# Two-layer attention and mixture-of-experts kernel: six shared tiles behind the routed ones, with layer 1's first normalised rows, its first products and the second batch's gather among them; low halves of layer 1's weights on POOL

## The chip, the cores and the metric

One core of one Trainium2 chip. The time is device microseconds of the whole kernel, from one launch. Engines are named as in the profile: PE (TensorE matmul), PEld (its weight loads), DVE (VectorE), ACT (ScalarE), POOL (GpSimd), SP (SyncE, which only issues DMAs here).

## What is computed

Four blocks in a row, on 8 batches of 512 tokens with 256 features:

```
x  = L0_attn(x)       # layer norm, 16-head causal attention
x  = x + L0_ffn(...)  # 8 routed experts, top 2 of a softmax router, plus one shared expert:
                      #   h = silu((x @ w1 + b1) * (x @ w3 + b3));  h @ w2 + b2   (hidden 352)
x  = L1_attn(x)       # z = sigmoid(x Wz + bz); a = 1 - z; b = z * (x Wh + bh)
                      # h_t = a_t h_(t-1) + b_t (a scan along tokens); sigmoid(h Wg + bg) * h
x  = L1_ffn(x)        # sigmoid router with groups, top 2 of 8 experts on a 128-wide latent,
                      # relu^2 experts, plus a shared relu^2 MLP of 1024
```

Products of fp32 accuracy are made from fp16 pairs: each operand is split in a high half (a rounded copy) and a low half (the rest), and three matmuls replace one: high by high, high by low, low by high.

## The kernel before, in words

Three phases, each a block of its own with one program per engine; a block ends when every engine has come to its end, and the next one starts behind that common barrier.

The first phase (L0_attn, router) runs until about 455 us. The second (`experts_phase`) handles tiles of 256 tokens. `over_experts` sets the order for all engines: 11 tiles of the shared expert (`HEAD_TILES`), then some 20 routed tiles, expert by expert, then 5 more shared tiles (`TAIL_TILES`, stages 0 to 4). A tile is the same work everywhere: PE `gate_up` (36 matmuls into banks 0 to 2, m = 0, 1, 2), ACT `bias1`, DVE `gated` (the product, which frees the bank for the next tile), ACT `hidden` (silu twice), DVE `hidden_lo`, and in the next tile's turn PE `out` of this one (18 matmuls), then DVE `total_y` and an SP store. PE's `gate_up(i, m)` waits for DVE's `gated(i-1, m)`.

Around this order lie pieces for others:
- In the head tiles DVE and POOL write one-hot matrices (`place` on DVE, L1638, eight per tile in tiles 0 to 7; `in_lane`, L1431, 64 on POOL, then two more, L1434). PE multiplies them (`table`, L1798) ahead of the last two head tiles, and the result, `tokens`, tells POOL which rows to gather for each routed tile: `fetch` (L1400 copies the tokens, L1404 gathers) and `move` (L1412, to `xg`), which PE transposes (`x_transposes`, L1730) one tile ahead, inside the last head tile for the first routed one.
- Layer 1's weights (8208 columns, `pack32`) come in 12 parts of 684 columns, loaded in the head tiles. ACT makes the high half of a part (`pack_part`, L1503), DVE the low half (L1631), in head tiles 1 to 10 and in tail stages 0 and 1.
- In the tail, POOL gathers the first batch's routed rows (L1453, eight gathers) once the last routed tile is stored. DVE adds them to the rows in `front.x2` and takes statistics (`first_sums` in stages 2 and 3, `first_statistics` in stage 3). POOL makes the inverse deviation (L1456 to L1461), ACT normalises (`first_normalise`, L1526, in stage 4 between `bias1` and `hidden`), PE transposes (`front_transposes`, L1778, in stage 4 behind `out` of stage 3). The tails of the engines: PE `out` of stage 4; ACT `xT_hi` (L1533); DVE `xT_lo` (L1668), `total_y` of stage 4, `first_slots(1)` (L1643, L1644).

The third phase (`layer1_phase`) runs eight batches, one `step` each. A step begins on PE with the router's logits (24 narrow matmuls, into l_sc on ACT), the latent `lat` (6 wide ones), `z0` (6), then `h0`, `z1`, `h1`, eight `up` products, and so on. On POOL, step b first gathers the routed rows of batch b+1 (L2018); DVE adds them in its step b (L2168). SP starts with three small loads of biases, waits for the last stored tile and loads the rows of the next batch (L1984).

## Time and profile before

| | |
|---|---|
| time, median of 3 runs | 1202.05 us (1201.46 to 1204.6) |
| profiled execution, its time | 1203.08 us |
| its span in the trace | 1201.3 us |
| PE busy | 1115.7 us (93%) |
| DVE busy | 894.9 us (74%) |
| ACT busy | 676.0 us (56%) |
| POOL busy | 531.2 us (44%) |
| mean granted clock of TensorE | 0.979 of full |

The page lists busy time by engine, the span in 40 slices, the chain of work that ended last, and groups of instructions. PE is busy nearly everywhere; what remains are places where it waits, and where its granted clock is at half. The answers below are cut to such places. A row of a timeline gives start, duration, engine, line, operation, what it writes and reads, how many are merged, and in brackets how long the engine stood idle before it and who released it. Matmuls overlap: one of 256 columns is shown with 0.27 us, the next begins 0.109 us later.

### The profile page before, as it was taken

How to read it: one execution, taken by the hardware profiler on the slowest of the kernel's cores; microseconds unless marked ns; L12 is line 12 of the kernel's file. 1: busy time of each engine (PE TensorE's matmuls, PEld its weight loads, DVE VectorE, ACT ScalarE, POOL GpSimd, SP SyncE). 2: the span in 40 equal slices, each digit the busy share in tenths (PEclk: the TensorE clock that was granted, in tenths of full speed). 3: DMA queues.
4: the chain of work that ended last, by engine and by line, in shares of the span. 5: the costliest groups of instructions: out<-in, count | busy, mean ns of one | idle time of the engine just before them, and what ended most of it. 6: DMA issues, size and time to landing. Idle time of an engine off the chain costs nothing. (4 is left out here: it accounts for less than half of the span.)

```text
span 1201.3 us, 26766 instructions
## 1 busy us (share of the span) xinstructions
PE 1115.7 (93%) x8899; PEld 747.5 (62%) x8931; DVE 894.9 (74%) x2219; ACT 676.0 (56%) x1464; POOL 531.2 (44%) x743
## 2 busy tenths in 40 slices
PE   6799999999999888998999999997999999999998
PEld 3345555555555437887998888983656646546555
DVE  5878797888887847975656667674886876877876
ACT  2355565565555554665656566654654654664653
POOL 6442433434333226854444343323646546447414
PEclk9799999999999999999999999997999999999999
DMA  6448435455334405755332453452241341331211
GB/s 162 108 90 227 99 68 110 98 98 107 62 85 93 82 18 186 218 162 155 113 101 79 126 159 122 127 155 74 89 141 35 107 140 35 105 106 63 95 45 62
DMA packets 105044, 129.36 MB, mean 108 GB/s; under 512 B 14976, under 2 KB 92736, under 8 KB 103936
## 3 DMA queue, kind: packets, MB, share of 16 engines
q1 hardware_dynamic: 93712, 109.08, 34.1%
q0 software_dynamic: 6912, 18.88, 5.6%
q10 hardware_dynamic: 4336, 0.34, 0.3%
q8 instruction: 46, 0.75, 0.3%
q14 instruction: 38, 0.31, 0.1%
HBM read 84.70 MB, written 43.38 MB: 107 GB/s over the span
## 5 line engine op out<-in xcount | busy, mean ns | idle before, releaser
L544 ACT ACTIVATE p<-bank 128x384 f32<-128x384 f32 (+1 forms) x384 | 191.6, 531 | 185.2 <-PE bank L957 136.1
L769 DVE TENSOR_REDUCE neg_max<-bank 128x1 f16<-128x384 f32 (+3 forms) x352 | 219.7, 640 | 65.9 <-PE bank L945 56.5
L463 POOL TENSOR_SCALAR_AFFINE_SELECT p<-p 128x256 f32<-128x256 f32 x256 | 104.5, 412 | 233.8 <-ACT p L544 233.1
L942 PE MATMUL bank<-k_stack,q_stack 96*128 96x384 f16 (+3 forms) x512 | 133.2, 312 | 23.4 <-DVE neg_max L769 13.0
L1404 POOL DMA_INDIRECT fetched<-xn_dram,token_now x80 | 81.2, 1014 | 42.9 <-POOL token_now L1400 30.7
L2033 POOL TENSOR_TENSOR up_lo<-up_sq,up_hi 128x512 f16<-128x512 f32 x32 | 43.8, 1398 | 120.8 <-ACT up_hi L2090 120.8
L2044 POOL TENSOR_TENSOR he_lo<-he_sq,he_hi 128x512 f16<-128x512 f32 x64 | 79.9, 1270 | 36.6 <-ACT he_hi L2133 36.6
L957 PE MATMUL bank<-q_stack,k_stack 97*128 97x512 f16 (+1 forms) x256 | 91.5, 360 | 3.1 <-ACT p L544 1.5
L1488 ACT ACTIVATE a<-xbank,b 128x256 f32<-128x256 f32 (+1 forms) x126 | 58.7, 469 | 52.3 <-PE xbank L151 48.8
L1576 DVE TENSOR_TENSOR h_lo<-h,h_hi 128x256 f16<-128x256 f32 x159 | 68.0, 431 | 24.3 <-ACT h_hi L1497 23.4
L975 PE MATMUL bank<-p,v_aug 128*32 128x512 f32 (+3 forms) x1024 | 83.9, 447 | 0.8 <-DVE o_rows L749 0.8
L942 PEld LDWEIGHTS bank<-k_stack,q_stack 96*128 96x128 f16 x512 | 45.2, 99 | 61.3 <-DVE neg_max L769 40.7
L149 PE MATMUL ybank<-l_xT_hi,pack_hi 128*128 128x512 f16 x208 | 79.9, 384 | 2.6 <-DVE up_sq L2247 2.6
L150 PE MATMUL ybank<-l_xT_lo,pack_hi 128*128 128x512 f16 x208 | 79.8, 384 | 0.0
L151 PE MATMUL ybank<-l_xT_hi,pack_lo 128*128 128x512 f16 x208 | 79.8, 384 | 0.0
L1495 ACT ACTIVATE h<-prod 128x256 f32<-128x256 f32 x159 | 64.8, 408 | 24.6 <-DVE prod L1570 19.5
L1570 DVE SCALAR_TENSOR_TENSOR prod<-xbank,b,a 128x256 f32<-128x256 f32 (+1 forms) x126 | 58.5, 477 | 24.8 <-ACT a L1488 20.3
L945 PE MATMUL bank<-mask_qk,identb 128*128 128x128 bf16 (+1 forms) x321 | 76.7, 239 | 0.0
L149 PE MATMUL ybank<-pack_hi,up_hi 128*128 128x256 f16 x256 | 69.8, 273 | 0.0
L150 PE MATMUL ybank<-pack_lo,up_hi 128*128 128x256 f16 x256 | 69.8, 273 | 0.0
L151 PE MATMUL ybank<-pack_hi,up_lo 128*128 128x256 f16 x256 | 69.8, 273 | 0.0
L2018 POOL DMA_INDIRECT rows_k<-y_routed_dram,slot x56 | 56.5, 1008 | 27.7 <-issue 15.9
(344 smaller groups left out, 3379.9 us busy)
## 6 DMA issues: line engine op xcount, KB each, us to landing
w_bc<-wT_dram SPq DMA_DIRECT2D x8, 2048.0 KB, 8.3
y_routed_dram<-y SPq DMA_DIRECT2D x37, 256.0 KB
w<-in_w SPq DMA_DIRECT2D x10, 704.0 KB
pack<-in_pack SPq DMA_DIRECT2D x12, 342.0 KB, 4.4
xr<-in_x SPq DMA_DIRECT2D x8, 512.0 KB, 6.9
xn_dram<-xn SPq DMA_DIRECT2D x8, 512.0 KB, 3.0
qk_hi_dram<-qk_hi SPq DMA_DIRECT2D x16, 256.0 KB, 2.7
qk_lo_dram<-qk_lo SPq DMA_DIRECT2D x16, 256.0 KB, 2.9
```

Source lines behind the costliest of these rows:

```text
L149: pe.matmul(out, hi_a(c), hi_b(c), start=first and x == 0, stop=False)
L150: pe.matmul(out, hi_a(c), lo_b(c), start=False, stop=False)
L151: mm = pe.matmul(out, lo_a(c), hi_b(c), start=False, stop=last and x == n - 1)
L463: pool.affine_select(out=diagonal, in_=diagonal, pattern=[[0, 2], [1, P]], compare_op=ALU.is_ge, fill=0.0, base=0, channel_multiplier=-1). ...
L544: act.activation(p32[:, s // GH % 2, s % GH, cols], s_bank[n][:, 0:cols.stop - cols.start], ACT.Exp).then_inc(p_exp.sem, 1)
L769: dve.tensor_reduce(neg_max[:, g % 2, 0:GH * TT].rearrange("p (h t) -> p h t", t=TT)[:, heads[0]:heads[-1] + 1, j], a_bank[c % 2][:, 0:len ...
L942: pe.matmul(to[:, at * w:(at + 1) * w], q_stack[0:STK, u, h0 + h, j * P:(j + 1) * P], k_stack[0:STK, u, h0 + h, 0:w], start=at == 0, stop= ...
L945: pe.matmul(diagonal, identb[:, :], mask_qk[:, 0:len(heads), :], start=False, stop=True).then_inc(a_psum.sem, 1)
L957: mm = pe.matmul(to[:, 0:S - n * P], k_stack[0:AUG, u, h, n * P:(n + 1) * P], q_stack[0:AUG, u, h, n * P:S], start=True, stop=True)
L975: mm = pe.matmul(out_bank[VW * h:VW * (h + 1), k * P:S], v_aug[:, b % 2, k, GH * (g % NG) + h, :], p32[:, g % 2, h, P_OFF[k]:P_OFF[k] + S ...
L1404: pool.indirect_dma_start(fetched[:, u, half, :], None, dram["xn"], bass.IndirectOffsetOnAxis(token_now[:, u, half:half + 1], 0)).then_inc ...
L2044: pool.tensor_tensor(he_lo[:, e, :], he_sq[:, e % EB, :], he_hi[:, e, :], ALU.subtract).then_inc(he_lo_s.sem, 1)
```

## The change

1. `TAIL_TILES` 5 to 6: one shared tile moves from the head (now 10) behind the routed tiles. `PACK_PARTS` = `HEAD_TILES` + 1 goes from 12 to 11, so a part has 747 columns.
2. The low halves of layer 1's weights go from DVE to POOL, one instruction a part: parts 0 to 4 behind POOL's one-hot work and ahead of its wait for `tokens`; 5 to 8 behind the last routed fetch; 9 and 10 behind the first batch's gather.
3. With six stages, sums and statistics stay in stages 2 and 3; `first_normalise` moves to stage 4 behind `hidden`; `front_transposes` is in stage 5 behind `out` of stage 4; ACT's and DVE's halves of the transposed rows in stage 5 behind `hidden` and behind `total_y`.
4. The second batch's slots (`first_slots(1)`) are made by DVE in stage 4, and POOL gathers that batch at the end of the second phase.
5. PE's logits, `lat` and `z0` of batch 0 go to the end of the second phase (`first_products`), ACT's sigmoid of the logits and `lat_hi` too; the three small loads go to its start.
6. To make room: the eight PSUM banks are shared by all phases, `x1` and layer 1's output rows take space held by the other phases, and some semaphores are merged (`w_hi` and `w_lo` count four instead of two, and the constants' start waits for five small POOL instructions instead of two).

```
-TAIL_TILES = 5
+TAIL_TILES = 6
+PACKED_EARLY = 5
...
-            pool.wait_ge(start, 2)
+            pool.wait_ge(made, 5)
...
         @block.gpsimd (experts)
+            def pack_part(n):
+                cols = bass.ds(n * PACK_PART, PACK_PART)
+                pool.wait_ge(pack_hi_s.sem, pack_hi_s.at(n))
+                pool.tensor_tensor(pack_lo[:, cols], pack32[:, cols], pack_hi[:, cols], ALU.subtract).then_inc(pack_lo_s.sem, 1)
...
+            for n in range(PACKED_EARLY):
+                pack_part(n)
             end = pool.value_load(bounds[0:1, E:E + 1], min_val=MIN_TILES, max_val=ROUTED_TILES)
             pairs = (end + 2) // 2
             pool.wait_ge(tokens_s.sem, 1)
...
+            for n in range(PACKED_EARLY, HEAD_TILES - 1):
+                pack_part(n)
             pool.wait_ge(front.slot_s.sem, front.slot_s.at(0))
             pool.wait_ge(y_stored.sem, y_stored.at(end + (HEAD_TILES - 1)))
...
+            for n in range(HEAD_TILES - 1, PACK_PARTS):
+                pack_part(n)
             pool.wait_ge(front.dve_ln.sem, front.dve_ln.at(0))
...
+            pool.wait_ge(front.x2_sum.sem, front.x2_sum.at(0))
+            pool.wait_ge(front.slot_s.sem, front.slot_s.at(1))
+            for t in range(TT):
+                for k in range(2):
+                    pool.indirect_dma_start(front.rows_k[:, t, k, :], None, dram["y_routed"], ...)
...
         @block.scalar (experts)
-                if stage == TAIL_TILES - 1:
-                    first_normalise()
                 for m in range(HM):
                     hidden(i, m)
+                if stage == TAIL_TILES - 2:
+                    first_normalise()
+                if stage == TAIL_TILES - 1:
+                    first_x_high()
...
             def tail(i, u):
+                act.wait_ge(front.lg_psum.sem, front.lg_psum.at(0))
+                act.activation(front.sc[:, :, :], ..., ACT.Sigmoid).then_inc(front.sc_s.sem, 1)
+                act.wait_ge(front.lat_psum.sem, front.lat_psum.at(0))
+                act.activation(front.lat_hi[:, :], bank[1][:, :], ACT.Copy).then_inc(front.lat_hi_s.sem, 1)
...
         @block.vector (experts)
-                if stage in (HEAD, TURN) and not is_int(i, 0):
-                    pack_part(i - 1)
-                elif stage in range(2):
-                    pack_part(HEAD_TILES - 1 + stage)
-                elif stage == TAIL_TILES - 3:
+                if stage == TAIL_TILES - 4:
                     first_sums(0)
                     first_sums(1)
-                elif stage == TAIL_TILES - 2:
+                elif stage == TAIL_TILES - 3:
                     first_sums(2)
                     first_sums(3)
                     first_statistics()
+                elif stage == TAIL_TILES - 2:
+                    dve.wait_ge(front.loaded.sem, front.loaded.at(0))
+                    dve.tensor_scalar(front.neg_bz[:, :], ...)
+                    first_slots(1)
+                elif stage == TAIL_TILES - 1:
+                    first_x_low()
...
         @block.tensor (experts)
+            def tail(i, u):
+                out(i, u)
+                first_products(i)
+
+            def first_products(i):
+                pe.wait_ge(front.xT_lo_s.sem, front.xT_lo_s.at(0))
+                pe.wait_ge(prod_s.sem, prod_s.at(i))
+                pe.wait_ge(pack_lo_s.sem, pack_lo_s.at(PACKED_EARLY - 1))
+                ...   # logits (24 narrow matmuls), lat (6), z0 (6)
...
         layer 1, all engines: what is named above is left out of step 0
-                if more:
+                if before and more:
                     gather(b + 1)
```

## Rows read from the trace of the kernel before

**Rows 1.** The page's first part: busy time and share of the span.

```profile
PE 1115.7 (93%) x8899; PEld 747.5 (62%) x8931; DVE 894.9 (74%) x2219; ACT 676.0 (56%) x1464; POOL 531.2 (44%) x743
```

**Rows 2.** Windows: stretch, length, busy time by engine, granted clock, DMA share, GB/s.

```profile
560.00:564.00 4.00, 4.00 (x24) 2.94 (x22) 2.23 (x6) 1.81 (x6) 0.00 (x0) 0.57 0.15 52
...
816.00:818.00 2.00, 0.13 (x2) 0.00 (x0) 1.62 (x6) 1.79 (x5) 0.00 (x0) 0.50 0.00 0
...
828.00:830.00 2.00, 2.00 (x7) 0.75 (x6) 1.01 (x7) 1.44 (x4) 1.39 (x3) 0.58 0.96 333
```

**Rows 3.** Timeline of PE from the last tile to layer 1's first steps.

```profile
815.04 1.09 PE L1778 MATMUL xbank<-identf,l_xn 128*128 128x128 f32 x8 [4.18 <-ACT l_xn L1526]
818.08 0.39 PE L149 MATMUL xbank<-w_hi,h_hi 128*128 128x256 f16 x1 [1.95 <-DVE y L1585]
...
823.92 0.17 PE L149 MATMUL ybank<-pack_hi,l_xT_hi 128*128 128x8 f16 x1 [1.81 <-PEq L1164]
...
829.63 0.41 PE L149 MATMUL ybank<-l_xT_hi,pack_hi 128*128 128x512 f16 x1
...
838.71 0.39 PE L149 MATMUL ybank<-l_xT_hi,pack_hi 128*128 128x512 f16 x1 [0.48 <-DVE up_sq L2247]
...
846.18 0.38 PE L149 MATMUL ybank<-hT_hi,pack_hi 128*128 128x512 f16 x1 [0.82 <-DVE up_sq L2247]
```

**Rows 4.** Timeline of DVE and ACT in the same stretch.

```profile
811.06 1.26 DVE L1570 SCALAR_TENSOR_TENSOR prod<-xbank,b,a 128x256 f32<-128x256 f32 x3
...
823.04 0.16 DVE L1644 COPY wk<-route_weights 128x8 f32<-128x8 f32 x1
...
828.86 0.19 DVE L2197 TENSOR_TENSOR sfc<-l_sc,corr 128x32 f32<-128x32 f32 x1 [1.59 <-ACT l_sc L2094]
...
830.40 0.69 DVE L2282 TENSOR_TENSOR lat_lo<-ybank,lat_hi 128x512 f16<-128x512 f32 x1
...
812.91 2.07 ACT L1526 ACTIVATE l_xn<-x,shift,l_rstd 128x256 f32<-128x256 f32 x4 [3.52 <-POOL shift L1461]
```

**Rows 5.** Timeline of POOL: first and last gather of batch 0, then the statistics.

```profile
794.07 0.94 POOL L1453 DMA_INDIRECT rows_k<-y_routed_dram,slot  x1 [18.71 <-DMA y_routed_dram<-y]
...
803.59 0.95 POOL L1453 DMA_INDIRECT rows_k<-y_routed_dram,slot  x1 [0.30 <-issue]
811.12 0.20 POOL L1456 TENSOR_TENSOR l_var_eps<-l_mv,eps_col 128x4 f32<-128x4 f32 x1 [6.58 <-DVE l_mv L1662]
```

**Rows 6.** The chain that ended last, in layer 1's first batch: start, duration, what.

```profile
833.48 2.77 DMA rows_k<-y_routed_dram,slot
```

**Rows 7.** Timeline of DVE in a middle head tile.

```profile
493.99 0.86 DVE L1631 TENSOR_TENSOR pack_lo<-pack,pack_hi 128x684 f16<-128x684 f32 x1
```

**Rows 8.** Timeline of PE in the head: a tile's start, the table, the first routed tile's transposes.

```profile
495.39 0.27 PE L149 MATMUL xbank<-turned,shared_in 128*128 128x256 f16 x1 [0.45 <-DVE prod L1570]
...
514.74 3.47 PE L1798 MATMUL xbank<-in_column,in_lane 128*128 128x114 f16 x64 [0.76 <-DVE prod L1570]
...
527.22 0.60 PE L1730 MATMUL xbank<-identf,xg 128*128 128x128 f32 x4
```

**Rows 9.** Timeline of POOL in the head.

```profile
502.97 1.76 POOL L1434 TENSOR_SCALAR in_column<-lanes,tail_at,tail_ids 128x114 f16<-128x114 f32 x2
518.70 0.18 POOL L1400 COPY token_now<-tokens 128x2 int32<-128x2 int32 x1 [13.97 <-DVE tokens L1719]
...
525.75 0.84 POOL L1412 COPY xg<-fetched 128x512 f32<-128x512 f32 x1
```

**Rows 10.** Three lines' instructions: count, shortest, median and longest duration in ns.

```profile
L2033 POOL TENSOR_TENSOR up_lo<-up_sq,up_hi x32: 1148/1158/1754, 846.5 to 1175.4; 128x512 f16<-128x512 f32 x32
...
L1431 POOL TENSOR_SCALAR in_lane<-lanes,pos_f x64: 590/600/1652, 461.9 to 502.4; 128x128 f16<-128x128 f32 x64
...
L1576 DVE TENSOR_TENSOR h_lo<-h,h_hi x159: 404/422/825, 464.8 to 816.9; 128x256 f16<-128x256 f32 x106, 96x256 f16<-96x256 f32 x53
```

**Rows 11.** Timeline of PE among the routed tiles: its longest wait there.

```profile
558.67 0.28 PE L149 MATMUL xbank<-w_hi,h_hi 128*128 128x256 f16 x1 [3.08 <-DVE y L1585]
```

More of the change, by code:

```diff
@@ L104, in sb @@
             return ctx.enter_context(nc.sbuf_tensor(name, shape, dt))
+        self.bank = [ctx.enter_context(nc.psum_tensor(f"bank{i}", [P, 512], F32)) for i in range(8)]
         self.xr = sb("xr", [P, TT, D])
+        self.x1 = sb("x1", [P, TT, D])
         self.x_loaded = Signal(nc, ctx, "x_loaded", 16)
@@ L225, in mix_phase @@
         run = route["run"]
-        bank = [ps(f"bank{i}", [P, 512]) for i in range(8)]
+        bank = carried.bank
         w_loaded = sig("w_loaded", 16 * 8)
-        wqkv_hi_s = sig("wqkv_hi_s", DC)
-        wqkv_lo_s = sig("wqkv_lo_s", DC)
-        w_hi = sig("w_hi", 2)
-        w_lo = sig("w_lo", 2)
+        w_hi = sig("w_hi", 4)
+        w_lo = sig("w_lo", 4)
         bq_scaled = sig("bq_scaled", 1)
@@ L1081, in constants @@
     with ExitStack() as own:
-        start = own.enter_context(nc.semaphore("const_start"))
         made = own.enter_context(nc.semaphore("const_made"))
@@ L1094, in _ @@
         def _(pool):
-            pool.memset(zeros[:, :, :], 0.0).then_inc(start, 1)
-            pool.memset(onesf[:, :], 1.0).then_inc(start, 1)
+            pool.memset(zeros[:, :, :], 0.0).then_inc(made, 1)
+            pool.memset(onesf[:, :], 1.0).then_inc(made, 1)
             pool.memset(c["ones_b"][:, :], 1.0).then_inc(made, 1)
@@ L1111, in _ @@
                                fill=MASKED, base=0, channel_multiplier=1).then_inc(made, 1)
-            pool.wait_ge(made, 7)
+            pool.wait_ge(made, 9)
     return c
@@ L1208, in experts_phase @@
         posf = sb("posf", [P, T // P, 2])
-        bank = [ctx.enter_context(nc.psum_tensor(f"xbank{i}", [P, 512], F32)) for i in range(8)]
+        bank = carried.bank
         front_bank = bank[6:8]
@@ L1806, in after_first, with tail, from_x @@
                     pe.nop(nofuse=True)
-            over_experts(pe, lambda: None, new_expert, tile, after_first, lambda e, u, first: None, table, out)
+            def tail(i, u):
+                out(i, u)
[4 more added lines that the diff above has]
+                pe.wait_ge(pack_lo_s.sem, pack_lo_s.at(PACKED_EARLY - 1))
+                def from_x(to, name, n):
+                    at, (_, width) = PACK[name]
+                    return three_products(pe, to, lambda c: pack_hi[:, at + c * width:at + c * width + n],
+                                          lambda c: pack_lo[:, at + c * width:at + c * width + n],
+                                          lambda c: front.xT_hi[:, c, :], lambda c: front.xT_lo[:, c, :], range(DC))
+                at = PACK["gate"][0]
+                for t in range(TT):
+                    tok = slice(t * P, (t + 1) * P)
+                    mm = three_products(pe, bank[0][:, t * E:(t + 1) * E], lambda c: front.xT_hi[:, c, tok],
+                                        lambda c: front.xT_lo[:, c, tok], lambda c: pack_hi[:, at + c * E:at + (c + 1) * E],
+                                        lambda c: pack_lo[:, at + c * E:at + (c + 1) * E], range(DC))
+                mm.then_inc(front.lg_psum.sem, 1)
+                from_x(bank[1][:, :], "fc1", LAT).then_inc(front.lat_psum.sem, 1)
+                from_x(bank[2][:, :], "wz", P).then_inc(front.z_psum.sem, 1)
+            over_experts(pe, lambda: None, new_expert, tile, after_first, lambda e, u, first: None, table, tail)
 PACK = {}
@@ L1859, in layer1_phase @@
         gh_hi, gh_lo = (sb(f"gh_{k}", [P, DC, S], F16) for k in ("hi", "lo"))
-        lat_hi, lat_lo = (sb(f"lat_{k}", [P, S], F16) for k in ("hi", "lo"))
-        sc = sb("l1_sc", [P, TT, E])
+        lat_lo = sb("lat_lo", [P, S], F16)
         sfc = sb("sfc", [P, TT, E])
@@ L1882, in layer1_phase @@
         comb_hi, comb_lo = (sb(f"comb_{k}", [P, S], F16) for k in ("hi", "lo"))
-        y = sb("l1_y", [P, TT, D])
-        bank = [ctx.enter_context(nc.psum_tensor(f"ybank{i}", [P, 512], F32)) for i in range(8)]
+        y = carried.turned[:, :, :, :, :].rearrange("p a b c n -> p (a b c n)").bitcast(F32)[:, 0:TT * D].rearrange("p (t d) -> p t d", t=TT)
+        bank = carried.bank
         out_bank, comb_bank = (bank[3], bank[4], bank[5], bank[7]), bank[6]
@@ L2092, in step @@
             def step(b, u, before, more):
-                act.wait_ge(lg_psum.sem, lg_psum.at(b))
-                act.activation(sc[:, :, :], ring("gate")[:, 0:TT * E].rearrange("p (t e) -> p t e", e=E),
-                               ACT.Sigmoid).then_inc(sc_s.sem, 1)
-                act.wait_ge(lat_psum.sem, lat_psum.at(b))
-                act.activation(lat_hi[:, :], ring("lat")[:, :], ACT.Copy).then_inc(lat_hi_s.sem, 1)
+                if before:
+                    act.wait_ge(lg_psum.sem, lg_psum.at(b))
+                    act.activation(sc[:, :, :], ring("gate")[:, 0:TT * E].rearrange("p (t e) -> p t e", e=E),
+                                   ACT.Sigmoid).then_inc(sc_s.sem, 1)
+                    act.wait_ge(lat_psum.sem, lat_psum.at(b))
+                    act.activation(lat_hi[:, :], ring("lat")[:, :], ACT.Copy).then_inc(lat_hi_s.sem, 1)
                 for c in range(DC):
```

109 lines of the change are left out of this document (56 added, 53 removed).

## The prediction, made before the changed kernel ran

> **What bounds the kernel now.** I read the page first: PE is busy 93% of the span [rows 1], so an edit pays only where PE stands idle, or works at half clock, or where work leaves PE. Then I cut the span into windows and looked at where the granted clock is 0.5, and at PE's timeline around each such place. The largest hole lies at the seam of the second and third phase. PE ends its last dense work at about 810.9 (the next row's start less its idle time, 815.04 less 4.18 [rows 3]), waits for ACT's normalised rows, makes eight transposes, waits 1.95 us, and has fallen to half clock (1.2 of 2.4 GHz) by 816.0 [rows 2]. It makes the last `out` at that level, stands 1.81 us at the barrier, and makes logits, `lat` and `z0` at half clock until 829.63, where `h0` starts and the clock is back [rows 2, 3]. At full clock the work of this stretch is 18 matmuls at 0.109 us (2.0), 24 narrow ones at 0.027 (0.65), 12 wide at 0.216 (2.6) and the transposes (0.6): 5.8 us of work in 18.7 us. Some 13 us is the most that can be won here.
>
> The other place is the head. There DVE, not PE, sets the pace: PE waits 0.45 us in a middle tile for DVE's product [rows 8], and DVE has 0.86 us of `pack_lo` in that tile ahead of the next product [rows 7].
>
> **The head, part by part.** Taking `pack_lo` from DVE frees 0.86 us a tile; PE can use its 0.45, and 0.16 more because matmuls overlap (0.27 less 0.11). Over six tiles that is up to 3.6 us, less at the ends; I take 3.2. With one head tile fewer (6.0) the table, at 514.74 before [rows 8], could start at 505.5. POOL's one-hot work ends at 502.97 + 1.76 = 504.7 [rows 9] and does not hold it. `tokens` follow 4 us after the table's start, at 509.5.
>
> But POOL now has five pack parts to do first, and every routed row waits behind them. The price of one is in no row; the nearest is the same instruction in layer 1 on 512 columns, median 1.158, longest 1.754 [rows 10]. By columns (747/512) that is 1.69 to 2.56 us, so five take 8.5 to 12.8. The median is nearer, as most of the 32 are close to it, but DVE has its own two-input subtractions there; I take 9.5. POOL then begins the token copy at 504.7 + 9.5 = 514.2. Before, it took from 518.70 to 526.6 until the rows lay in `xg` [rows 9], 7.9 us, and PE's transposes of them came at 527.22 [rows 8], in time for PE. Now they can come at 514.2 + 7.9 + 0.2 = 522.3. PE would be there 8.5 us after it took up tiles again (527.22 less 518.70 [rows 8, 9]), at 518. So DVE's 3.2 us are spent, and PE stands about 4 us inside the last head tile. This is the wait that takes the place of the one removed: transposes 4.9 us earlier than before (527.22 to 522.3), with a tile of 5.9 us (54 matmuls at 0.109) still to be done behind the routed ones. Net +1.0 us.
>
> Such a wait also costs clock. The one wait of 3.08 us among the routed tiles [rows 11] was followed by a mean granted clock of 0.57 over 4 us [rows 2]: half that time's work is lost, 1.7 us. A wait of 4 us should do the same; I add 1.7. Head: +2.7, between -0.3 (median parts and no fall of the clock) and +6.0 (longest parts, +4.3, and the fall).
>
> The Trainium skill has a rule that speaks against this part: SBUF — State Buffer, section Who interferes with whom, says that a VectorE instruction with two SBUF inputs and a GpSimd instruction that reads SBUF hold each other off for a whole instruction. The trace agrees in kind: `h_lo`, 0.422 us in the median, has one of 0.825 [rows 10]. By that rule the parts would be held by some five `h_lo` of 0.42, five parts take 10.6 and the head costs +3.8 instead of +2.7.
>
> **The routed tiles.** Nothing changes in them but what follows from their start; POOL's parts 5 to 8 (4 x 1.9 = 7.6) fall in its 18.71 us of idle time ahead of the first gather [rows 5]. If that cover were gone the gather would be late by the excess. Parts 9 and 10 (3.8) lie behind that gather and ahead of the inverse deviation; POOL stood idle for 6.58 us there [rows 5].
>
> **The seam.** I write its times as if the head cost nothing; then all stages begin 5.9 us earlier and stage 5 stands where stage 4 stood. DVE's product of stage 4, at 811.06 behind sums and statistics [rows 4], comes at 805.2; PE would like it at 804.8 and waits 0.85 for it. `hidden` of stage 4 on ACT ends at 807.5, normalising takes 2.07 [rows 4] until 809.6, while PE is still in stage 5: the wait of 4.18 is gone. Behind that normalising, `bias1` of stage 5 is queued, so its product comes at 811.7 on DVE, its `hidden` ends at 812.8, `total_y` of stage 4 at 813.9. PE: `out` of stage 4 and the transposes until 812.1, 1.9 us idle, `out` of stage 5 from 814.0 to 815.9, then logits, `lat` and `z0` until 819.3. ACT's halves (812.8 to 813.9) and DVE's (to 815.2) are there in time. The table load for the sigmoid goes ahead of the barrier, beside PE.
>
> The second gather: DVE's slots are made at 809.1, I allow 0.7 us until POOL's first gather is under way, and eight gathers take 10.5 (794.07 to 804.54 [rows 5]): POOL ends at 820.2 and is the last. The barrier opens 0.6 us after it (before, 823.04 + 0.16 to 823.92 [rows 3, 4]): 820.8. There `h0` starts, instead of at 829.63: 8.8 us. Three of them are the barrier's move, 5.7 the products that no longer lie behind it.
>
> What is late next? DVE has 2.2 us from `sfc` to the end of `lat_lo` (828.86 to 831.09 [rows 4]), now from the barrier on, and `z1` waits for it: 1 us of PE. But PE waited later for DVE in any case (0.48 at 838.71, 0.82 at 846.18 [rows 3]), because DVE stood behind the second batch's rows, whose last landing took 2.77 us from 833.48 [rows 6]. They now land by 823, before DVE wants them at 827. Followed through, `up3` comes at 829.9 for 838.71 and the first gate product at 837.4 for 846.18. The 8.8 us stay. Seam: -8.8.
>
> **At nothing:** three small loads in SP's prologue (1.3 us, SP then waits for PE's first tile anyway); the longer start condition of the constants (under 0.2 us of POOL, while the first DMAs are in flight); the shared banks; `neg_bz` and slots on DVE in stage 4 (0.3 us, ahead of stage 5's product, which waits for ACT until later).
>
> **The sum.** -8.8 + 2.7 = -6.1 us. Against the profiled execution, 1203.1, that gives 1197.0; it lies 1.0 above the median of the runs, so the median should be 1202.05 - 6.1 = 1196.0.
>
> **Rivals.**
> (a) The clock falls at the seam too. For it: 1.9 us of idle time behind transposes; against: before, it fell only after 4.18 us of idle time, transposes and further idle time [rows 2, 3]. PE would end the products about 2.1 us later and hold the barrier: 1198.0 or somewhat more.
> (b) The parts cost their median, 8.5 us, and the short wait leaves the clock alone: head about 0, 1193.2.
> (c) DVE and POOL hold each other off: parts of 2.56, head +6.0, 1199.3. By the Trainium skill's rule on the shared port pair, above, the price would lie between forecast and this.
> (d) The seam's gain is lost: gather or normalising come late (the slots' place on DVE, a slower gather), POOL ends at 826 instead of 820.2 and `h0` starts at 826.6: 1201.8.
> (e) Slower: the same queue on POOL, at a price from which it decides. With the clock's 1.7 the head eats the seam's 8.8 once five parts take 15.6 us, 3.1 each; slower by over 0.3% from 3.8 each. For it: a one-hot instruction of 0.600 in the median took 1.652 once; against: the longest subtraction is 1.5 times its median [rows 10]. At 4.2 each the time is 1207.5.
>
> **Chances.** Forecast 0.35, (a) 0.20, (b) 0.21, (c) 0.12, (d) 0.08, (e) 0.04. The range is from (b) less 2.5 to (c) plus 1.7, 1190.7 to 1201.0. About 0.3%, 3.6 us, is what a measurement of this kernel can tell from no change. Below 1198.4 lie nearly all of the forecast and of (b), half of (a), a little of (c): faster 0.70. Slower is (e) and an unknown: 0.05. Same 0.25.
>
> **What would show it.** Right, if POOL's first `token_now` stands behind five `pack_lo` at about 514, PE waits about 4 us for `xg` ahead of its first transposes and the clock falls there; if head tiles come every 5.9 to 6.0 us; if, from the transposes in stage 5 to `h0`, there are some 9 us instead of 14.6 (815.04 to 829.63), with POOL's gather last before the barrier; and if DVE no longer waits for `rows_k` in batch 0. Wrong, if the low halves take under 1.5 or over 2.6 us, if PE finds `xg` ready, if the barrier waits for PE, or if later batches get longer.

## The result, and the profile after

The changed kernel takes 1209.85 us in the median (before: 1202.05), a ratio of 1.0062 with a 95% interval of 1.0047 to 1.0077. The forecast was 1196.0: wrong in size and in sign, since the whole interval lies above 1. The profiled execution has a span of 1207.6 us for 1201.3. Page of the changed kernel, busy time and granted clock in 40 slices:

```profile
PE 1110.9 (92%) x8899; PEld 746.7 (62%) x8931; DVE 898.3 (74%) x2207; ACT 675.4 (56%) x1463; POOL 541.2 (45%) x754
PEclk8799999999999999999999999998999999999999
```

PE works 5 us less than before [rows 1], and the span is 6.3 longer: PE stands more. It does so in two places.

**The head.** POOL's and DVE's timelines of the changed kernel (start, duration in us, engine, line, operation, what it writes and reads, count, and in brackets the idle time before it and what ended it):

```profile
500.63 7.83 POOL L1432 TENSOR_TENSOR pack_lo<-pack,pack_hi 128x747 f16<-128x747 f32 x5
521.08 0.19 POOL L1414 COPY token_now<-tokens 128x2 int32<-128x2 int32 x1 [12.62 <-DVE tokens L1759]
528.14 0.62 POOL L1426 COPY xg<-fetched 128x512 f32<-128x512 f32 x1
```

```profile
501.23 8.82 DVE L1677 TENSOR_SCALAR in_column<-lanes_half,pos_f,ids 128x116 f16<-128x116 f16 x8
509.97 1.26 DVE L1612 SCALAR_TENSOR_TENSOR prod<-bank,shared_b,a 128x256 f32<-128x256 f32 x3
513.46 1.83 DVE L1677 TENSOR_SCALAR in_column<-lanes_half,pos_f,ids 128x116 f16<-128x116 f16 x8
```

The queue I feared isn't there: POOL is through with its five parts at 508.5 and then waits 12.62 us for the tokens (13.97 before [rows 9]). What is late is DVE. Eight places, which take 1.83 us together in the tile behind, take 8.82 beside the five parts. The row for the line (shortest, median, longest ns) shows that one of them alone does it:

```profile
L1677 DVE TENSOR_SCALAR in_column<-lanes_half,pos_f,ids x64: 298/316/7281, 465.9 to 515.0; 128x116 f16<-128x116 f16 x64
```

It starts at 501.23 and ends at 508.51, when the last part of POOL ends; the seven behind it take 300 ns each. PE's timeline, and the windows (length, busy us of PE, weight loads, DVE, ACT, POOL, then the clock) of the changed kernel:

```profile
515.51 5.08 PE L1838 MATMUL bank<-in_column,in_lane 128*128 128x116 f16 x64 [10.72 <-issue]
```

```profile
505.00:520.00 15.00, 4.49 (x56) 4.52 (x57) 9.92 (x24) 2.66 (x7) 3.46 (x3) 0.66 0.32 103
815.00:829.00 14.00, 9.24 (x90) 6.91 (x88) 5.38 (x16) 6.90 (x16) 7.65 (x8) 1.00 0.49 150
829.00:840.00 11.00, 6.00 (x15) 2.11 (x16) 4.95 (x30) 1.95 (x4) 0.00 (x0) 0.53 0.15 48
```

PE waited 10.72 us ahead of the table and then made most of it at half clock, 5.08 us for 3.47 [rows 8]. The table starts at 515.51, 0.8 later than before [rows 8] although a tile fewer is ahead of it.

**The seam.** PE, POOL and DVE of the changed kernel:

```profile
811.97 0.28 PE L152 MATMUL bank<-turned,w_hi 128*128 128x256 f16 x1 [1.25 <-DVE prod L1612]
817.87 1.04 PE L1818 MATMUL bank<-identf,l_xn 128*128 128x128 f32 x8
820.11 0.28 PE L152 MATMUL bank<-w_hi,h_hi 128*128 128x256 f16 x1 [1.20 <-DVE y L1627]
834.00 0.59 PE L152 MATMUL bank<-l_xT_hi,pack_hi 128*128 128x512 f16 x1 [8.56 <-PEq L1174]
852.54 0.38 PE L152 MATMUL bank<-hT_hi,pack_hi 128*128 128x512 f16 x1 [0.82 <-DVE up_sq L2297]
```

```profile
816.01 1.03 POOL L1493 DMA_INDIRECT rows_k<-y_routed_dram,slot  x1 [2.64 <-issue]
824.84 0.94 POOL L1493 DMA_INDIRECT rows_k<-y_routed_dram,slot  x1 [0.30 <-issue]
```

```profile
841.69 1.66 DVE L2218 SCALAR_TENSOR_TENSOR x<-rows_k,wk,xr 128x256 f32<-128x256 f32 x4
```

Up to the products all is as forecast: transposes and `out` without ACT's wait, products at full clock (1.00 from 815 to 829), and later DVE's sums without a wait for rows. Then PE stands 8.56 us at the barrier. POOL's last gather is issued by 825.78, `h0` starts 8.2 us later. What lies between is no work and is in no row above. It is the DRAIN of POOL, an instruction of its sequencer at the end of the phase, which the records show from 819.10 on, while the last gathers are still being issued. From the sequencers' records (start us, ns, engine, event) of both kernels:

```
before:  812.64  7535 GpSimd DRAIN        823.51  130 Sync DRAIN      823.80 barrier opens
after:   819.10 14601 GpSimd DRAIN        823.66  129 Sync DRAIN      833.88 barrier opens
```

Before, POOL's last instruction ended at 812.88 and its DRAIN at 820.17, 7.3 us later, unseen, since SP's store held the barrier until 823.6. Now it ends at 833.70, 7.9 behind the last gather, and by then every other engine is done (PE's own DRAIN ends at 825.49).

How long the DRAIN outlasts POOL's last instruction goes by how many gathers POOL issued in the phase. All phases of all the traces of this case fall in five groups (gathers issued in the phase, us from the end of POOL's last instruction to the end of its DRAIN, traces):

```
 0 gathers  0.06 to 0.07   first phase, all 17 traces
48 gathers  4.00 to 4.01   third phase, second batch gathered in the second phase, 12 traces
56 gathers  4.66           third phase, second batch gathered in layer 1, 5 traces
88 gathers  7.28 to 7.29   second phase, second batch gathered in layer 1, 5 traces
96 gathers  7.92 to 7.93   second phase, second batch gathered there, 12 traces
```

That is about 0.083 us a gather. What POOL did last doesn't matter: with 88 it was a `tensor_tensor` or a memset, with 48 and 56 a `tensor_tensor` some 80 to 90 us behind the last gather.

### The profile page after: what moved, and what is told of

The parts are those of the page before. It is cut to its first block and busy times, and to the rows that moved or that the text cites. A ratio compares the mean times of both kernels' runs of the same rounds, so it can differ in the third digit from the quotient of the medians.

```text
span 1207.6 us, 26775 instructions
## 1 busy us (share of the span) xinstructions
PE 1110.9 (92%) x8899; PEld 746.7 (62%) x8931; DVE 898.3 (74%) x2207; ACT 675.4 (56%) x1463; POOL 541.2 (45%) x754
## 5 line engine op out<-in xcount | busy, mean ns | idle before, releaser
L940 PE MATMUL bank<-k_stack,q_stack 96*128 96x384 f16 (+3 forms) x512 | 133.0, 312 | 21.8 <-DVE neg_max L767 13.4
L152 PE MATMUL bank<-l_xT_hi,pack_hi 128*128 128x512 f16 x208 | 80.1, 385 | 10.7 <-PEq L1174 8.6
L1521 ACT ACTIVATE a<-bank,b 128x256 f32<-128x256 f32 x129 | 59.8, 468 | 51.6 <-PE bank L154 48.0
L1618 DVE TENSOR_TENSOR h_lo<-h,h_hi 128x256 f16<-128x256 f32 x159 | 72.9, 462 | 19.7 <-ACT h_hi L1530 18.8
L153 PE MATMUL bank<-l_xT_lo,pack_hi 128*128 128x512 f16 x208 | 80.0, 385 | 0.0
L154 PE MATMUL bank<-l_xT_hi,pack_lo 128*128 128x512 f16 x208 | 79.8, 384 | 0.0
L1612 DVE SCALAR_TENSOR_TENSOR prod<-bank,b,a 128x256 f32<-128x256 f32 x129 | 60.0, 477 | 24.5 <-ACT a L1521 18.7
L154 PE MATMUL bank<-pack_hi,up_lo 128*128 128x256 f16 x256 | 69.8, 273 | 0.0
L153 PE MATMUL bank<-pack_lo,up_hi 128*128 128x256 f16 x256 | 69.8, 273 | 0.0
L152 PE MATMUL bank<-pack_hi,up_hi 128*128 128x256 f16 x256 | 69.8, 273 | 0.0
L2311 DVE SCALAR_TENSOR_TENSOR rw<-bank,w_bc 128x512 f32<-128x512 f32 x64 | 43.3, 687 | 33.2 <-PE bank L154 31.5
```

The source lines that it names most:

```text
L152: pe.matmul(out, hi_a(c), hi_b(c), start=first and x == 0, stop=False)
L153: pe.matmul(out, hi_a(c), lo_b(c), start=False, stop=False)
L154: mm = pe.matmul(out, lo_a(c), hi_b(c), start=False, stop=last and x == n - 1)
L940: pe.matmul(to[:, at * w:(at + 1) * w], q_stack[0:STK, u, h0 + h, j * P:(j + 1) * P], k_stack[0:STK, u, h0 + h, 0:w], start=at == 0, stop= ...
```

## The experiments

The experiments ran on four chips. On one of them the kernel before takes 1203 us, close to the 1202 of the first measurement; on the other three it takes 1241 to 1246, mostly because there a batch of layer 1 takes 51 to 54 us for 46.5. Ratios are to the kernel before on the same chip. They stand beside the changed kernel's 1.0062 and, measured again on the faster chip, 1.0050. On the slower chips the changed kernel itself never ran, so a ratio from there isn't clear evidence against those two; what an edit did is read from its trace.

**First four: each cause undone, and a probe (a slower chip).**

Packs behind the fetch loop:

```diff
-            for n in range(PACKED_EARLY):
-                pack_part(n)
...
-            for n in range(PACKED_EARLY, HEAD_TILES - 1):
+            for n in range(HEAD_TILES - 1):
```

> The changed kernel with POOL's five early pack parts moved from behind its one-hot rows to behind the loop that fetches the routed rows, where the other four already run (nine there; the stretch before gather 1 was 7.60 us idle after four). Theory A (POOL's back-to-back subtractions held DVE's place for 7.28 us in head tile 6, and that is most of what the head lost): the eight places of every head tile take 1.8 to 2.5 us, the table moves from 515.5 back to 509 to 510 us, the first routed transposes from 529.6 to about 523, TensorE's clock doesn't fall before the table, and the median goes from 1209.9 to about 1202.5 us (1201 to 1204). It doesn't come to the forecast's 505.5 for the table, because with one head tile fewer the table waits for tile 7's own place, which comes behind DVE's h_lo and y. Theory B (place was held by something else in that stretch, the lost head tile itself for one): the eight places still take 6 to 9 us and the time stays within 2 us of 1209.9. Theory C (the packs' place costs as much behind the loop): head repaired, but gather 1 waits for POOL and comes 1 to 3 us later than 793.2, so the sums and the seam lose what the head gains.

Ratio 1.0039 (1.0019 to 1.0060), where theory A had the kernel level with the one before. In the head the hold is gone, as theory A says: places take 1.84 us and the table starts at 510.71. The clock still fell, against theory A, since PE still waited 3.91 us ahead of the table (0.54 from 509 to 516). And the nine parts in a row took DVE's time at the new place:

```profile
775.48 15.91 POOL L1432 TENSOR_TENSOR pack_lo<-pack,pack_hi 128x747 f16<-128x747 f32 x9 [3.27 <-issue]
```

```profile
777.30 5.10 DVE L1616 TENSOR_TENSOR h_lo<-h,h_hi 128x256 f16<-128x256 f32 x3
782.33 0.74 DVE L1625 TENSOR_TENSOR y<-bank,b 128x256 f32<-128x256 f32 x2
805.89 4.11 DVE L1690 SCALAR_TENSOR_TENSOR x<-rows_k,wk,x 128x256 f32<-128x256 f32 x2
```

Three `h_lo` of 0.42 take 5.10 us, and two sums of 0.5 take 4.11 beside parts 9 and 10 (806.01 to 809.18). `y`, which reads PSUM, keeps its 0.74. I had foreseen a late gather (theory C). It was 2.3 us late, but waited for a store and not for POOL's parts; the loss was DVE's.

Gather 2 back in layer 1's first step, alone and with the edit above:

```diff
-            pool.wait_ge(front.x2_sum.sem, front.x2_sum.at(0))
...
-                if before and more:
+                if more:
                     gather(b + 1)
```

> The changed kernel with the second batch's gather moved back to the start of layer 1 (first step), the rest as it is. Theory A (POOL's DRAIN at the end of a phase ends about 7.3 us after POOL's last instruction when the phase had DMAs that GpSimd issues, and the gather at the end only pushed it out of the shelter of the other engines): POOL's last instruction is shift at about 813.4, its DRAIN ends by 821, the barrier opens for SP's store or TensorE's products at 826 to 826.5 instead of 833.8, h0 starts there (7.5 us sooner), and the median falls from 1209.9 to about 1202.5 us, minus what DVE then waits for the rows: gather from 826.5, last rows at about 838 to 840, against DVE's sums that in the changed kernel started at 841.7 and would start at 834.2 now; so 1202.5 to 1207, near 1205. Theory B (the barrier waited for the gather's transfers or their descriptors, not for a drain of fixed length): the same sooner barrier, so this run doesn't tell B from A; the drain probe does. Theory C (something else opened the barrier at 833.8, for one TensorE's products or its dropped clock): barrier stays at 832 to 834 and the time at 1209 to 1211.

> The changed kernel with both edits, packs behind the loop and gather back in layer 1. If the head's lock and the end's drain are two separate losses on the path, the gains add up: 1209.9 less 7.4 less 2.5 to 7.4, that is 1195 to 1200 us, faster than the kernel before (1202.05). If they shared one cause or one hid behind the other (the clock after the head for one), the sum comes short: 1201 or above.

Ratios 1.0056 (1.0030 to 1.0082) and 1.0047 (1.0029 to 1.0064). Both miss what I had expected; for the two edits together that was a kernel faster than the one before. POOL's DRAIN ended at 828.90 in the first of them, ahead of ACT's at 833.18 and PE's at 833.85, and PE passed the barrier with 0.34 us of waiting. Much of the gain was lost again a few us later. Of that run, DVE and PE:

```profile
846.53 1.67 DVE L2211 SCALAR_TENSOR_TENSOR x<-rows_k,wk,xr 128x256 f32<-128x256 f32 x4 [6.09 <-DMA rows_k<-y_routed_dram,slot]
```

```profile
826.23 1.04 PE L1811 MATMUL bank<-identf,l_xn 128*128 128x128 f32 x8
834.13 0.38 PE L152 MATMUL bank<-l_xT_hi,pack_hi 128*128 128x512 f16 x1 [0.34 <-PEq L1174]
848.86 0.61 PE L152 MATMUL bank<-l_xT_hi,pack_hi 128*128 128x512 f16 x1 [5.42 <-DVE up_sq L2290]
857.61 0.38 PE L152 MATMUL bank<-hT_hi,pack_hi 128*128 128x512 f16 x1 [0.43 <-DVE up_sq L2290]
```

Ahead of the barrier the gather costs POOL's drain, behind it DVE's wait for the rows. The two prices aren't equal. From the first row of the transposes to `h0` it is 7.9 us here (826.23 to 834.13) for 16.1 in the changed kernel (817.87 to 834.00), and from `h0` to the first gate product 23.5 (834.13 to 857.61) for 18.5: 3.3 of the 8.2 us are kept. The ratio doesn't show them. In this trace 294.1 us lie between the first routed transposes and those of the normalised rows, for 288.3 in the changed kernel's, and which part of that is the chip's isn't known.

The drain by itself, on the kernel before:

```diff
+            pool.wait_ge(front.slot_s.sem, front.slot_s.at(1))
+            pool.memset(ones8[:, :], 1.0)
```

> The kernel before, with one tiny memset on POOL at the end of its experts phase that waits for DVE's copies of the second batch's slots (823.2 us), nothing else. No gather is outstanding by then (the last one's rows were in by about 808). Theory A (drain of a fixed length behind POOL's last instruction, in a phase with GpSimd's own DMAs): POOL's DRAIN ends 7.3 us after the memset, at about 830.8; the barrier, at 823.8 before, opens at about 831 and the median rises from 1202.05 to about 1208 (1206.5 to 1209.5). Theory B (the drain of the changed kernel waited for the gather's transfers): the memset's DRAIN is over in under 1 us, the barrier opens at about 824.3 and the time stays within 1 us of 1202.05.

Ratio 1.0039 (1.0001 to 1.0077), by its trace theory A:

```profile
827.40 0.10 POOL L1463 MEMSET ones<- 128x8 f32 x1 [10.38 <-DVE wk L1646]
```

```profile
835.07 0.17 PE L149 MATMUL ybank<-pack_hi,l_xT_hi 128*128 128x8 f16 x1 [8.84 <-PEq L1164]
```

A memset of 0.1 us, with no gather under way, moved the barrier to 834.95: POOL's DRAIN ended at 834.78, 7.3 us behind the memset, and SP's, the next latest, at 827.77. So the barrier waits for the drain, and the drain is as long with no transfer to wait for.

**Second four: ways around (the faster chip).** The changed kernel again; parts 0 to 8 one each behind routed pairs 2 to 10; the rows of batch 1 in tiles of their own, so that four of their gathers run ahead of the inverse deviation and four right behind it; both:

```diff
+            for n in range(HEAD_TILES - 1):
+                two(2 + n)
+                pack_part(n)
...
+            gather_next(range(2))
             pool.wait_ge(front.dve_ln.sem, front.dve_ln.at(0))
...
-            pool.wait_ge(front.x2_sum.sem, front.x2_sum.at(0))
...
+            gather_next(range(2, TT))
```

> The changed kernel again, unedited, beside the next three on one chip, since the first four runs came from a chip on which the kernel before takes 1241.1 us (its layer 1 batches take 51 to 54 us instead of 46.5). Every theory: slower than the kernel before by 0.3 to 0.9% on either chip, POOL's DRAIN at the end of the experts phase 14.6 us, one place of 5 to 9 us in head tile 6 or 7.

> The changed kernel with the nine pack parts of POOL taken out of both blocks (five ahead of the tokens, four behind the fetch loop) and put one each behind the fetches of routed pairs 2 to 10. Theory A (POOL's subtraction holds a DVE operation whose operands all lie in SBUF until it ends, at most one part of 1.6 to 1.8 us when parts stand alone, and the routed stage is TensorE's with DVE busy 0.65 of it): head repaired as in the run with the packs behind the loop (table at about 510, transposes about 5 us sooner than in the changed kernel), and no loss at 775 to 791 us, where nine parts in a row stretched DVE's h_lo and w_lo; 4 to 8 us less than the changed kernel on the same chip. Theory B (any h_lo held in the routed stage reaches TensorE, since out waits for it): each part costs 0.5 to 1.6 us of the span, 5 to 14 us in all, and the time comes out at or above the changed kernel's.

> The changed kernel with the second batch's rows gathered into tiles of their own (they lie where the lower half of in_lane was, and layer 1's he_hi later), so that no gather has to wait for the sums: four of the eight gathers right behind the packs that follow gather 1 (from about 806.7), four behind shift (from about 813.5); nothing else changed. Theory A (the end of the phase was held by POOL's drain, 7.3 us and more behind its last gather): the last gather ends its issue at about 818.5 instead of 825.8, the drain at 826, beside SP's last store; the barrier opens at 826 to 826.5 instead of 833.8 and DVE finds the rows there, so 6 to 7.5 us less than the changed kernel on the same chip. Theory B (gathers in flight lengthen the drain beyond 7.3 us): barrier later than 828. Theory C (four gathers ahead of the rstd chain delay normalise): front transposes up to 1 us later.

> Both edits, packs spread over the routed pairs and rows of the second batch early. If head and end are separate losses: the sum of the two gains, 10 to 15 us under the changed kernel on the same chip and 4 to 8 us (0.3 to 0.7%) under the kernel before. If they hide behind one another: no better than the better one of the two.

Medians 1211.5, 1207.0, 1199.4 and 1198.1 us for 1203.4 before; ratios 1.0050 (1.0022 to 1.0079), 1.0035 (1.0017 to 1.0052), 0.9965 (0.9953 to 0.9976) and 0.9967 (0.9949 to 0.9985). So the gather's place at the end, with the drain and the clock behind it, is the larger loss: 12 us by the medians, where I had expected 6 to 7.5, and 10 to 12 by the ratios. Its trace beside the changed kernel's first one accounts for 9.3 of them, 7.4 ahead of `h0` and 1.9 behind it. Spreading the packs gains 4.5 us with the drain in place, inside the 4 to 8 expected, and 1.2 without it; neither is clear of the ratios' intervals. Both edits together give 13.4, of 10 to 15 expected. The changed kernel again: DVE's places and, later, its sums, both held, though no single place for more than one part (1.64 us), as in the probe below:

```profile
503.61 6.47 DVE L1677 TENSOR_SCALAR in_column<-lanes_half,pos_f,ids 128x116 f16<-128x116 f16 x8
805.51 4.20 DVE L1692 SCALAR_TENSOR_TENSOR x<-rows_k,wk,x 128x256 f32<-128x256 f32 x2 [0.37 <-DMA rows_k<-y_routed_dram,slot]
```

With the packs spread, PE's table is made 6.4 us sooner than in the changed kernel, still behind a wait:

```profile
509.10 4.70 PE L1842 MATMUL bank<-in_column,in_lane 128*128 128x116 f16 x64 [3.91 <-issue]
```

With the rows early, PE at the seam, and POOL's last gather:

```profile
818.72 1.04 PE L1829 MATMUL bank<-identf,l_xn 128*128 128x128 f32 x8
827.47 0.38 PE L152 MATMUL bank<-l_xT_hi,pack_hi 128*128 128x512 f16 x1 [1.18 <-PEq L1177]
```

```profile
818.31 0.95 POOL L1492 DMA_INDIRECT lane_rows<-y_routed_dram,next_slot  x1 [0.30 <-issue]
```

From transposes to `h0` it is now 8.75 us (818.72 to 827.47), the 9 that I had forecast, against 16.1 in the changed kernel and 14.6 before. The DRAIN again ends 7.9 us behind the last gather (819.26 to 827.18), and the clock stays at full level behind the barrier (1.00 from 829 to 840).

**Third four: the table's wait, the price of the move, a probe (a slower chip).** Ten places a tile instead of eight, on top of both edits of before; the changed kernel with all low halves on DVE; the version with all three mends and parts 9 and 10 on DVE; and, on the kernel before, five dummy subtractions on POOL behind its one-hot rows:

```diff
-                for n in range(PLACED_A_TILE * i, PLACED_A_TILE * (i + 1)):
+                for n in range(10 * i, min(10 * (i + 1), PLACED_BY_DVE)):
```

```diff
+            for n in range(5):
+                pool.wait_ge(pack_hi_s.sem, pack_hi_s.at(n))
+                pool.tensor_tensor(scratch[:, n, :], pack32[:, bass.ds(n * PACK_PART, PACK_PART)], pack_hi[:, bass.ds(n * PACK_PART, PACK_PART)], ALU.subtract)
```

> The previous version (packs spread over the routed pairs, second batch's rows early) with DVE's 64 places made ten a head tile in tiles 0 to 5 and four in tile 6, instead of eight in tiles 0 to 7. Theory A (with POOL out of the way the table still waits 3.91 us because, with one head tile fewer, it waits for the places of the very tile ahead of it): the wait ahead of the table falls from 3.91 to under 1.3 us, the table starts at 505.5 to 507.5 instead of 509 to 510, the clock doesn't fall there, and the median goes 3 to 6 us under that of the version before it (1198.1 on a chip where the kernel before takes 1203.4), ratio to the kernel before 0.992 to 0.994. Theory B (the wait is for another thing, DVE's h_lo and prod of the tile ahead, or the time saved is lost again to POOL's tokens and gathers): wait stays over 3 us or the routed transposes don't move.

> The changed kernel with all eleven low halves made by DVE, as in the kernel before (one a head tile and two in the first shared tiles of the end), everything else as changed; this prices the move to POOL by itself. Theory A (the move's price by the locks is more than DVE's relief is worth): DVE's head tile goes back from 5.8 to about 6.5 us (8 tiles, about 5 us), the table's wait shrinks, the held places (6 to 9 us) and held sums or h_lo at 805 to 811 us are gone, and the median comes out 1 to 5 us under the changed kernel's, near 1206. Theory B (the relief is worth more): 2 or more us above the changed kernel's. The drain stays at the end (7.9 us behind the last gather) by either.

> The version with packs spread, rows early and places sooner, and with the last two low halves (stages 0 and 1 of the end) made by DVE. Theory A (those two parts on POOL, back to back beside DVE's sums and h_lo, cost up to 3 us of held DVE in some executions): 0 to 3 us under the version without this edit and less scatter; the four gathers ahead of the rstd chain then also end 3.2 us sooner. Theory B: no measurable difference.

> The kernel before with five subtractions of pack width added on POOL behind its one-hot rows, into scratch (nothing reads them), where POOL was idle from 504.7 to 518.7 us; they take about 1.5 us each, to about 512. Theory A (back-to-back POOL subtractions hold a DVE operation with all operands in SBUF): DVE's places, h_lo or pack parts at 504.8 to 512 are held for 1.5 to 7 us each, the table starts 3 to 7 us later than 514.7, and the median rises by 3 to 8 us from 1202 (ratio 1.0025 to 1.0065). Theory B (what held DVE's place in the changed kernel came with its other edits): DVE's operations keep their lengths within 10%, and the time stays within 1 us of the kernel before's.

Places sooner: 0.9920 (0.9894 to 0.9947), with the table's first half without a wait and at full clock (the second half follows at 510.18):

```profile
508.51 1.82 PE L1853 MATMUL bank<-in_column,lane_rows 128*128 128x116 f16 x32
```

Packs on DVE: 1.0044 (1.0023 to 1.0065), not to be told from the changed kernel's two ratios. Parts 9 and 10 on DVE: 0.9967 (0.9943 to 0.9992), no gain. Its PE stood 6.6 us in all inside the first shared tile behind the routed ones, in waits that the profile puts to nothing. Between 788 and 812 such waits come to 1.3 to 6.6 us in every trace of the slower chips and to 0.5 us at most in those of the faster one and of the first measurement; why is open. The probe: 1.0037 (1.0013 to 1.0060), and its timelines:

```profile
503.59 7.29 DVE L1642 TENSOR_SCALAR in_column<-lanes_half,pos_f,ids 128x114 f16<-128x114 f16 x8
```

```profile
512.20 0.37 PE L149 MATMUL xbank<-turned,shared_in 128*128 128x256 f16 x1 [5.43 <-DVE prod L1574]
520.63 3.48 PE L1802 MATMUL xbank<-in_column,in_lane 128*128 128x114 f16 x64
```

POOL's and DVE's single instructions in that stretch (start us, ns) show how it goes: one place between two of POOL's parts.

```
504.39 1482 GpSimd TENSOR_TENSOR
504.39 1523 Vector TENSOR_SCALAR
505.82 1477 GpSimd TENSOR_TENSOR
505.83 1519 Vector TENSOR_SCALAR
507.26 1474 GpSimd TENSOR_TENSOR
507.27 1519 Vector TENSOR_SCALAR
```

The table starts at 520.63 for 514.74 [rows 8]: POOL's subtractions alone, read by nobody, cost the kernel before 5.9 us there. They held five places, none for longer than one part, where the changed kernel's five parts held a single one. The eight places take 7.29 us here and 8.82 there, so 5.5 and 7.0 us are lost, most of the parts' own time by either way.

**Last three: how the head's loss splits (a slower chip).** The best version again; the same with all low halves on DVE; the changed kernel with places sooner alone.

> The version with packs spread over the routed pairs, second batch's rows early and places sooner, unedited, in more rounds, since its first measurement rests on five runs. Theory A: ratio to the kernel before 0.990 to 0.995. Theory B (the 0.992 was owed to few runs): 0.995 to 0.998, no better than without the sooner places.

> The same, but with all eleven low halves made by DVE as in the kernel before: rows of the second batch early, places ten a tile, no subtraction of packs on POOL. It tells what the move of the low halves to POOL is worth once nothing is held by it. Theory A (DVE's head tile at 6.5 us or more against 5.8 is paid in full, seven or eight times 0.7): 4 to 6 us above the version with packs spread. Theory B (what DVE gains in the head, POOL's parts take back in the routed stage by holding h_lo): within 2 us of it.

> The changed kernel with the places made sooner (ten a tile) and nothing else, POOL's five early parts where they are. Theory A (two causes in the head: places held by POOL, and a table that waits for the places of the tile just ahead): the held place is still there in tile 6 (three to seven us), but none comes behind it in tile 7, so the table starts at 510 to 512 instead of 515.5 and the time falls 3 to 5 us below the changed kernel's (1206 on the chip where the kernel before takes 1203). Theory B (the lock alone counts): table still at 514 or later and no gain over 1 us.

Ratios 0.9953 (0.9931 to 0.9976), 1.0003 (0.9980 to 1.0027), 1.0024 (1.0001 to 1.0046). The best version is faster than the kernel before; how much, two measurements put at 0.5 to 0.8% (the one with more runs at 0.5). Whether the sooner places add anything to the 0.9967 without them, the times don't show. By the medians the move to POOL is worth 5.7 us (1236.3 for 1242.0) once the parts are spread: on DVE the tiles come every 6.95 us (products at 486.51, 493.45, 500.40), and the table starts 2.8 us later, counted from the end of the first phase. Some of the rest may be the unexplained waits, 3.9 us longer in this trace. And the table's order is a cause beside the hold. Of the last run, the held places in tile 5 and the table, now without a wait though the hold is there:

```profile
499.07 5.27 DVE L1677 TENSOR_SCALAR in_column<-lanes_half,pos_f,ids 128x116 f16<-128x116 f16 x10
```

```profile
512.50 3.48 PE L1838 MATMUL bank<-in_column,in_lane 128*128 128x116 f16 x64
```

## Why the prediction was wrong, step by step

Against the profiled execution I forecast -6.1 us and it was +6.3. The 12.4 between them lie in three stretches, taken from the rows above. Transposes in stage 5 ended at 818.91; by the working 812.1 and the head's 2.7, so 4.1 too early. From there to `h0`: 8.7 forecast, 15.1 measured, 6.4. From `h0` to the first gate product: 16.6 forecast (820.8 to 837.4), 18.5 measured (834.00 to 852.54), 1.9. Together 12.4.

- **The head tile: right.** DVE's products came at 486.19, 491.97 and 497.74, 5.8 us apart, and PE took up tiles at 486.92, 492.82 and 498.72, the 5.9 of the forecast.
- **Price of a part: forecast 1.9, measured 1.6** (7.83 for five). Over-sized, and harmless. The low end of the head's range is off too: its own terms give 0.0 to -0.1 for parts at their median, not -0.3.
- **The queue ahead of the tokens: didn't happen.** The token copy at 514 stood on a table at 505.5. With the table at 515.5, POOL was idle again for 12.62 us. I looked for the wait that takes the place of the one removed, and put it on the wrong engine.
- **The table could start at 505.5: the step that failed in the head,** twice over. First, the hold. I had it as a stretch of POOL's parts, 10.6 us for five or, in rival (c), 2.56 for each, and asked only for what POOL loses. It was DVE that was held, its place for 7.28 us. Second, the order. The table waits for all places, and those of tile 7 come behind that tile's `h_lo` and `y`; with 11 head tiles another tile lay between. Without any hold this alone leaves 3.91 us (packs spread), and ten places a tile take it away. PE's wait ahead of the table was 10.72 us, and the clock fell as I had said it would for a wait in the head: 0.66 in the mean from 505 to 520, 0.50 from 509 to 519.
- **What the head cost.** Rows were moved to `xg` at 528.14 for 525.75 [rows 9]: 2.4 later, with a tile of 5.9 us still to be done behind the routed ones, 8.3 instead of 2.7. By the transposes of stage 5 the difference is 4.1, so 1.5 of it was won back on the way; where, the rows here don't say.
- **The seam up to the products: right,** in order and in length; the run with the rows early gives 8.75 us from transposes to `h0` for my 9.
- **The barrier opens 0.6 us behind POOL's gather: the step that failed at the seam.** The 0.6 was read between DVE's last copy [rows 4] and PE's first product, but it was SP that came last to that barrier (its DRAIN ended at 823.64), and DVE's own DRAIN ends 0.05 us behind its last copy. I carried the figure over to POOL, whose DRAIN outlasts its last work by 7.3 to 7.9 us in this phase. It was in the trace of before, 7.5 us long, and was hidden by SP's store; moving POOL's last work from 812.9 to 825.8 took the cover away. The eight gathers moved with it made the drain itself 0.6 us longer. The drain probe shows the drain without the change, and the run with the rows early shows the gain when it ends sooner.
- **Clock behind the barrier: not foreseen.** PE stood 8.56 us, and the clock was 0.53 from 829 to 840. That is the 1.9 us of the third stretch: with the rows early and the clock at 1.00 the same stretch takes 16.6 (827.47 to 844.09), as forecast. Rival (a) had the fall among the products; there the clock held.
- **DVE no longer waits for the rows: right.** Its sums at 841.69 had no wait; with the gather in layer 1 they waited 6.09 us.
- **The rivals.** (c) was nearest in the head, by its mechanism, with the victim reversed. (d) had POOL ending at 826, which it did, and priced 0.6 us behind it. (e) put the slower outcome on a price per part of 3.8, which is excluded. The slower result came from two mechanisms that I had not listed; the 0.05 given to slower stood on (e) and on an unknown, and it was the unknown.

The Trainium skill, SBUF — State Buffer, section Who interferes with whom, has the rule: a VectorE instruction with two SBUF inputs contends with a GpSimd instruction that reads SBUF, one in a two-port mode, which `tensor_scalar` can enter, contends with GpSimd too, and whichever comes first keeps the other fully blocked for the whole of its instruction. The runs agree on who is held (places, `h_lo`, sums) and who is not (`y`, `prod`, with an operand in PSUM). They go beyond it in one thing: a place was held for five of POOL's instructions, not one. I had used only its first half, and only on POOL's price.

## What to carry to other kernels

Before giving an idle engine more work, ask whom it holds while it works, not only who waits for its result: list the other engine's instructions in that stretch and whether their operands all lie in the shared memory; single parts spread out cost little here, the same five in a row nearly their sum. Before moving an engine's last instruction to the end of a phase, look for that engine's drain in the trace of before, at what hid it, and at how many gathers it follows. When a loop loses an iteration, check every wait whose slack was that iteration.

## What the runs showed of the hardware that I had not expected

- POOL's DRAIN at the end of a phase outlasts POOL's last instruction by about 0.083 us for each gather issued in the phase: 0.1 us for none, 4.0 for 48, 4.7 for 56, 7.3 for 88, 7.9 for 96. It is the same on all four chips, whatever the last instruction was and however long ago the last gather.
- A DVE instruction of 0.30 us was held for 7.28 us by five `tensor_tensor` of POOL in a row, not for one of them only; in other executions each place was held for one part (1.52 us in the probe, 1.64 in the changed kernel again). POOL's one-hot `tensor_scalar`, as dense, did far less in these traces: eight places beside them took 2.3 us for 1.84, none over 0.44.
- The same program takes 3% longer on three of four chips, nearly all of it in layer 1, whose batches take 51 to 54 us for 46.5. The traces show where: in the drain probe ACT takes up a batch's logits at 891.88, though PE was through with them at 885.6, and PE then waits for it. What ACT waits for the profile only calls remote; no trace of the faster chip has that wait, and its cause is open.

```profile
891.88 0.20 ACT L2096 ACTIVATE l_sc<-ybank 128x32 f32<-128x32 f32 x1 [9.11 <-remote]
892.14 0.61 PE L149 MATMUL ybank<-l_xT_hi,pack_hi 128*128 128x512 f16 x1 [3.90 <-ACT l_sc L2096]
```
